# A shared ring of four PSUM banks divided in two, and score operands of 128 rows: two graph layers over 128 graphs

## The reference, cut to what matters

```python
# layer 0
h = maximum(layernorm(x), 0)
x = x + adj @ (h @ weight) + bias
# layer 1: eight attention heads, scores are a query term plus a key term
h = maximum(layernorm(x), 0)
feat = (h @ fc_w + fc_b)                    # 8 heads x 256
q, k = feat @ q_w + q_b, feat @ k_w + k_b   # one number per node and head
a = softmax(leaky_relu(q + k.T + (1 - adj) * NEG, 0.01))
x = x + sigmoid(concat_heads(a @ feat) @ fp_w + fp_b + h)
```

## Time and profile before

| what | value |
|---|---|
| time, median of 3 runs | 1684.23 us (1683.88 to 1689.58) |
| profiled execution, its own time | 1687.05 us |
| its span, first to last instruction | 1685.3 us |
| granted TensorE clock, mean | 0.992 of full speed |
| busy TensorE / VectorE / ScalarE / GpSimd | 98% / 80% / 71% / 52% |
| DMA, mean over the span | 33 GB/s |

### The profile page before, as it was taken

How to read it: one execution, slowest core, us unless ns; L and a number is a source line. 1 busy time by engine, 2 the same in 40 slices (tenths; PEclk the granted TensorE clock), 3 DMA queues, 4 the chain that set the end, 5 groups by cost and what they waited for, 6 DMA issues and landing times.

```text
span 1685.3 us, 33165 instructions
## 1 busy us (share of the span) xinstructions
PE 1645.1 (98%) x10176; PEld 1373.4 (81%) x10176; DVE 1342.5 (80%) x4719; ACT 1194.4 (71%) x3603; POOL 875.2 (52%) x1180
## 2 busy tenths in 40 slices
PE   5699999999999999999999999999999999999998
PEld 4588888888888888888888888888888888888887
DVE  1388888888888888888888888888888888888886
ACT  1277777777777777777777777777777777777775
POOL 1245555555555555555555555555555555555553
PEclk9799999999999999999999999999999999999999
DMA  4001011001001101101101101000100110110000
GB/s 145 25 20 39 19 37 37 25 31 37 29 27 37 37 19 37 37 19 37 37 19 37 37 19 37 37 21 35 37 25 31 37 37 19 37 37 19 38 13 13
DMA packets 20260, 55.64 MB, mean 33 GB/s; under 512 B 2896, under 2 KB 3280, under 8 KB 19856
## 3 DMA queue, kind: packets, MB, share of 16 engines
q1 hardware_dynamic: 20240, 55.40, 9.1%
HBM read 38.62 MB, written 16.78 MB: 33 GB/s over the span
## 4 chain that ended last, share of the span: by engine, by line
PE 97%; issue 1%; DMA 1%; POOL 1%; DVE 1%; SPq 0%; ACT 0%; POOLq 0%; DVEq 0%
PE gbank L217 44%; PE ybank L217 22%; PE front L217 14%; PE gbank L316 7%; PE sbank L309 6%; PE front L285 2%; PE gbank L233 2%; DMA kqb<-q_b_dram 1%; SPq L187 0%; PE front L238 0%; PE front L241 0%; DVE att L496 0%; POOL att L769 0%; DVE att L489 0%; ACT att L627 0%
## 5 line engine op out<-in xcount | busy, mean ns | idle before, releaser
L769 POOL TENSOR_TENSOR att<-att,rinv 128x512 f32<-128x512 f32 x256 | 266.3, 1040 | 548.2 <-DVE rinv L501 548.2
L620 ACT ACTIVATE g_hi<-gbank 128x512 fp32r<-128x512 f32 x512 | 304.0, 594 | 234.0 <-PE gbank L217 234.0
L217 PE MATMUL gbank<-m_hi,hT_lo 128*128 128x512 f32 x1024 | 424.4, 414 | 0.0
L627 ACT ACTIVATE att<-att 128x128 f32<-128x128 f32 x1024 | 396.5, 393 | 26.3 <-DVE att L496 26.3
L217 PE MATMUL gbank<-m_hi,hT_hi 128*128 128x512 f32 x1024 | 406.8, 397 | 0.0
L217 PE MATMUL gbank<-m_lo,hT_hi 128*128 128x512 f32 x1024 | 403.6, 394 | 0.0
L469 DVE TENSOR_TENSOR g_lo<-gbank,g_hi 128x512 fp32r<-128x512 f32 x512 | 344.8, 673 | 13.8 <-ACT g_hi L620 13.8
L217 PE MATMUL ybank<-g_hi,pT_lo 128*128 128x256 f32 x1024 | 307.4, 300 | 0.0
L217 PE MATMUL ybank<-g_lo,pT_hi 128*128 128x256 f32 x1024 | 288.4, 282 | 0.0
L217 PE MATMUL ybank<-g_hi,pT_hi 128*128 128x256 f32 x1024 | 287.7, 281 | 0.0
L476 DVE TENSOR_TENSOR pT_lo<-gbank,pT_hi 128x512 fp32r<-128x512 f32 x256 | 176.0, 687 | 91.5 <-ACT pT_hi L634 91.5
(11 more groups left out here) (94 smaller groups left out, 3054.2 us busy)
## 6 DMA issues: line engine op xcount, KB each, us to landing
g_in<-graph_dram SPq DMA_DIRECT2D x64, 512.0 KB, 3.3
out_dram<-late SPq DMA_DIRECT2D x64, 256.0 KB, 2.0
late<-fc_wT_dram SPq DMA_DIRECT2D x2, 1024.0 KB, 6.1
fp_sb<-fp_w_dram SPq DMA_DIRECT2D x1, 2048.0 KB, 11.3
w_f<-w_dram SPq DMA_DIRECT2D x1, 256.0 KB, 10.3
hmask<-head_mask_dram SPq DMA_DIRECT2D x1, 256.0 KB, 10.9
b_row<-bias_dram SPq DMA_DIRECT2D x1, 128.0 KB, 10.8
c_row<-fp_b_dram SPq DMA_DIRECT2D x1, 128.0 KB, 10.8
```

The lines of the kernel that those rows point to most:

```text
L217: mm = pe.matmul(out_ap, w, m, start=first and n == 0, stop=last and n == len(terms) - 1)
L620: act.activation(g_hi[j][:, s], gbank[tenant(RING, 4, ("g", n), p)[0]][:], ACT.Copy).then_inc(a_g[n], 1)
L627: e = act.activation(a[:, s], a[:, s], ACT.Exp, scale=-1.0, bias=a[:, CH + h:CH + h + 1], accum_out=esum[j][c][:, h:h + 1])
L769: gp.tensor_tensor(a, a, rinv[j][c][:].unsqueeze(2).broadcast_to([P, HC, P]), ALU.mult)\
```

## The change

The ring of four `gbank` becomes two rings of two. `gbank` keeps two banks and serves the eight projections alone, in their old order; a new `pbank` of two serves the four transposed blocks, in their old order. A projection thus waits until VectorE has read the projection two places earlier, and a transpose until it has read the block two places earlier. The queues of all engines keep their orders. Beside that the operands of the score matmuls get 128 rows: `lq`, `rk` and `hmask` are allocated with 128 partitions, the mask is loaded whole (its array has 128 rows, those from 64 on are zero), and the setup writes rows 64 to 127 of `lq` and `rk` with zeros once. What is written per pair (rows 0 to 31 of `rk`, rows 32 to 63 of `lq`) stays as it is.

```diff
-RING = ((("g", 6), -1), (("t", 1), -1), (("g", 7), -1), (("t", 2), -1), (("t", 3), -1), (("g", 2), 0),
-        (("g", 0), 0), (("g", 3), 0), (("g", 1), 0), (("t", 0), 0), (("g", 5), 0), (("g", 4), 0))
+GRING = ((6, -1), (7, -1), (2, 0), (0, 0), (3, 0), (1, 0), (5, 0), (4, 0))
+TRING = ((1, -1), (2, -1), (3, -1), (0, 0))
...
-        hmask = sb("hmask", [ROWS, H, P])
+        hmask = sb("hmask", [P, H, P])
...
-        lq = [two(f"lq{k}", [ROWS, P], F32R) for k in range(2)]
-        rk = two("rk", [ROWS, H, P], F32R)
+        lq = [two(f"lq{k}", [P, P], F32R) for k in range(2)]
+        rk = two("rk", [P, H, P], F32R)
...
-        gbank = [psum(f"gbank{k}", [P, BANK]) for k in range(4)]
+        gbank = [psum(f"gbank{k}", [P, BANK]) for k in range(2)]
+        pbank = [psum(f"pbank{k}", [P, BANK]) for k in range(2)]
...
-                             (coef[:], row_coef), (hmask[:], head_mask[0:ROWS]),
+                             (coef[:], row_coef), (hmask[:], head_mask),
...
-            def ring_free(key, p):
-                bank, (what, n), pair = tenant(RING, 4, key, p)
-                if has(pair) and what == "g":
-                    pe.wait_ge(v_g[n // 2], 2 * pair + 1 + G_RANK[n])
-                elif has(pair):
-                    pe.wait_ge(v_pT[n], pair + 1)
+            def projection_free(n, p):
+                bank, m, pair = tenant(GRING, 2, n, p)
+                if has(pair):
+                    pe.wait_ge(v_g[m // 2], 2 * pair + 1 + G_RANK[m])
                 return gbank[bank]
+
+            def probabilities_free(n, p):
+                bank, m, pair = tenant(TRING, 2, n, p)
+                if has(pair):
+                    pe.wait_ge(v_pT[m], pair + 1)
+                return pbank[bank]
...
             def project(p, q, n):
-                bank = ring_free(("g", n), p)
+                bank = projection_free(n, p)
...
-                bank = ring_free(("t", NC * j + c), p)
+                bank = probabilities_free(NC * j + c, p)
...
-                        e = dve.tensor_copy(lq[k][j][:], coef[0:ROWS, j:j + 1].broadcast_to([ROWS, P]))
+                        e = dve.tensor_copy(lq[k][j][:], coef[:, j:j + 1].broadcast_to([P, P]))
```

More of the change, by code:

```diff
@@ L467, in g_low @@
                 j, s = n // GC, slice((n % GC) * BANK, (n % GC + 1) * BANK)
-                bank = gbank[tenant(RING, 4, ("g", n), p)[0]]
+                bank = gbank[tenant(GRING, 2, n, p)[0]]
                 dve.tensor_tensor(g_lo[j][:, s], bank[:], g_hi[j][:, s].bitcast(F32), ALU.subtract)\
@@ L474, in pT_low @@
                 hs = slice(c * HC, (c + 1) * HC)
-                rows = gbank[tenant(RING, 4, ("t", NC * j + c), p)[0]][:].rearrange("p (h n) -> p h n", h=HC)
+                rows = pbank[tenant(TRING, 2, NC * j + c, p)[0]][:].rearrange("p (h n) -> p h n", h=HC)
                 dve.tensor_tensor(pT_lo[j][:, hs, :], rows, pT_hi[j][:, hs, :].bitcast(F32), ALU.subtract)\
@@ L619, in g_high @@
                 j, s = n // GC, slice((n % GC) * BANK, (n % GC + 1) * BANK)
-                act.activation(g_hi[j][:, s], gbank[tenant(RING, 4, ("g", n), p)[0]][:], ACT.Copy).then_inc(a_g[n], 1)
+                act.activation(g_hi[j][:, s], gbank[tenant(GRING, 2, n, p)[0]][:], ACT.Copy).then_inc(a_g[n], 1)
             def exp(p, j, c):
```

## The result

The changed kernel takes 1838.04 us (median of 4 runs, 1835.4 to 1839.13) against 1685.58 before, measured beside it: ratio 1.0898, 95% interval 1.0874 to 1.0923. Its profiled execution spans 1836.9 us, 151.6 more than before. The forecast was +124 (1809), the range 1785 to 1858.

A forecast was written before the change was run, and what follows sets the result against it. TensorE, busy 98% of the span, was taken as the bound. Projection 6's 0.94, projection 7's 0.90 and restart 0.10 gave +1.94 us a pair, x 64 = +124, predicting 1809 us; range 1785 to 1858.

The forecast's parts named there:

- The row surcharge: Around TensorE's score matmuls: changing between 64 and 128 rows costs 1.47 us a pair, which 128 rows everywhere remove.
- the cases: For 128-row score matmuls on TensorE: a plain step (gain 1.47 us a pair) or nothing changed (gain 0).
- Projection 3: On TensorE: it waits 0.31 us for VectorE's g_low 2, starting at 811.58; restart makes the second matmul 0.10 late.
- The working's step of 0.60 from leaky 0 to mask_min 1: On VectorE: mask_min 1 follows leaky 0 by 0.60 us, its 0.23 of idle gone.
- Projection 6: On TensorE: it waits 2.00 us for VectorE's g_low 5, starting at 821.40, 0.94 us late against before.
- Projection 7: On TensorE: waiting for VectorE's g_low 4, it starts 4.15 us behind projection 6 instead of 3.25, 0.90 more.
- the bounds that the forecast gave itself: Total time 1770 to 1828 us, from no projection 3 wait and free restarts (+85) to 0.3 more latency (+143).
- the first rival: Row surcharge stays around TensorE's scores: +2.65 us a pair, +170, 1854 us; chance 0.08.
- The clock: Rival: TensorE's clock falls with the new waits, a slow projection 6 costs 1.4 us, +90, 1899; chance 0.05.
- the prediction's own last sign: On TensorE: the prediction is wrong if matmuls behind the gaps show 0.63 us.
- The mask's load: In setup: growing from 256 to 512 KB costs nothing to 1.4 us; nothing was taken.
- The race for leaky 0: VectorE against GpSimd's residual: taken as won; rival says lost, g_low 2 about 1.3 us later, +83, 1892; chance 0.07.

The follow-up runs named there:

- experiment 1: Kernel before with only the score operands (`lq`, `rk`, `hmask`) widened to 128 rows, ring of four kept: 1596.26 us, ratio 0.9461.
- Experiment 4: Changed kernel with VectorE's g_low 5 moved right behind pT_low 0 and g_low 4 ahead of pT_low 1: 1621.45 us, ratio 0.9617.
- Experiment 3: Changed kernel with VectorE's g_low 5 moved right behind pT_low 0, nothing else: 1681.84 us, ratio 0.997.
- experiment 6: Changed kernel with VectorE's g_low 5 moved ahead of stats1 and mean1, 0.96 us sooner: 1753.08 us, ratio 1.0402.
- experiment 2: Changed kernel with score operands put back to 64 rows, so the divided rings alone: 1893.88 us, ratio 1.1233.
- experiment 8: Changed kernel with four extra, unread 512-column matmuls ahead of the wait for projection 6: 1816.59 us, ratio 1.0759.
- experiment 5: Changed kernel with only VectorE's g_low 4 moved ahead of pT_low 1: 1832.8 us, ratio 1.0862.
- 9: Kernel of experiment 5 with four extra, unread 512-column matmuls ahead of the wait for projection 6: 1757.6 us, ratio 1.0415.
- 7: Kernel of experiment 4 with VectorE's g_low 2 also moved ahead of mask_min 1: 1623.96 us, ratio 0.9631.
- 10: Kernel of experiment 7 with VectorE's g_low 0 also moved ahead of leaky 1 and inverse 0: 1598.79 us, ratio 0.9473.

## Why the prediction was right, point by point

**The row surcharge.** Right in mechanism and size: 1.43 us a pair against 1.47 (experiment 1). That the time still rose by 9% is because the second half of the change cost more than this one gave. What separated the cases was the pair of score matmuls back to back. Within the changed kernel the gain is real but of use only as far as projection 1; behind that, projection 6 hangs on VectorE.

**Projection 3.** Wait as forecast (start 811.60 against 811.58). Experiment 4, where it alone is left, prices it with its restart: 24.00 - 23.60 = 0.40, forecast 0.41 (0.31 and 0.10). The working's step of 0.60 from leaky 0 to mask_min 1 stands in no row shown; the changed kernel has 0.62 there.

**Projection 6.** The largest term, and right: it starts 8.30 behind projection 1 (909.67 to 917.97), forecast 8.32, and 1.84 us of idle show of the 2.00 us counted from start to start. Experiment 3 shows the cause by moving a single line, and experiment 6 by moving it part of the way.

**Projection 7.** 4.17 behind projection 6, forecast 4.15. The term was 0.90, and experiments 3 and 4 differ by 24.90 - 24.00 = 0.90.

**The sum and the range.** +1.97 a pair against the forecast +1.94, so 124 is what the undisturbed pairs lost. The measured 152 has 28 more, and 1838 lies above the bounds that the forecast gave itself, 1770 to 1828. It lies within the range of 1785 to 1858 only because that was widened for the first rival (1854), a surcharge that stays, and experiment 1 shows that it went. That part was luck.

**The clock, sized wrong.** I kept it as a rival of its own, either in all pairs (+90) or in none, with 0.05. It was neither: it fell in 13 of the 63 steady distances, at 1.5 us each, which the working had as 1.4. By the prediction's own last sign, matmuls behind the gaps that show 0.63, it was wrong in these 13 pairs. The step that failed in it is "no row falls behind so short a wait" as a reason for nothing; the trace of before has no wait of 2 us in a steady pair at all, so it could not exclude it. Measured, the term is 20 us (13 x 1.5) in place of 0.

**Setup and tail.** The mask's load, which I took as nothing, cost about its upper bound: TensorE's first matmul is at 20.40 instead of 19.04, and at 20.2 to 20.7 in all kernels with the large mask, 19.30 with the small one in experiment 2. The mask itself lands no later than before (15.45 against 15.98); the last small load, of q_b, which that matmul waits for, is issued at 10.32 instead of 8.42. The other 2 us before the first pair are not settled. Scores 0 of the first pair start at 79.5 to 85.7 over these profiles, with the same mask in both extremes. TensorE ran 79 matmuls between 24.3 and 37.5 in the earliest kernel (experiment 6) and 42 in the latest (experiment 8), which fits a clock that rises at different times in setup. The 2.6 us of the tail beyond the pair's 1.97 have two sources that the timeline shows: without `aggregate` between, projection 3 waits 1.49 us in the last pair, and the clock falls once more.

**The race for leaky 0.** Won in all pairs, as taken; before, it was lost in 35 of 64. The residual on GpSimd takes 1.68 (median) for it, forecast 1.8. Experiment 2 shows what a loss costs in the divided ring with 64 rows, 0.6 a pair; the 1.3 that the rival put on it with 128 rows was not tested.

## What to carry to other kernels

Before a ring of buffers is shortened or divided, list for each user its new predecessor and read from the trace when that one is given back: a release that lies 1.6 us behind the user's start costs nothing while another buffer is between, and all of it when there is none. The cure was not more banks but VectorE's order: work that frees a bank goes ahead of work that has slack. In this kernel a matmul of 64 rows between matmuls of 128 left the weight loads on both its sides exposed (0.37 and 0.24 us of idle loader); padding it with zero rows cost nothing per pair.

## What the runs showed of the hardware that was not expected

Behind a wait of 1.84 us in an otherwise dense stream of TensorE the granted clock fell to its 1.2 GHz level for 3.4 us, at 1.5 us a time: in 13 of 63 steady pairs of the changed kernel, and in 48 of 63 when the pair was 0.9 shorter (experiment 5). No steady pair fell where the wait was cut to 0.85 or 0.91 (experiments 6, 8, 9), nor in the kernels with shorter waits or none (1, 3, 4, 7, 10). Extra matmuls that nobody reads, put into such a wait, gave back 21 and 75 us.

The length of a wait does not decide alone. In experiment 2 none of 63 waits of 1.49 us ahead of projection 6 was followed by a fall, while 7 falls came right behind a wait that shows 0.53 us ahead of projection 3. What ran ahead differs: there it is `aggregate` and scores 2, ahead of projection 6 it is projection 4. Whether that is what counts was not tested.
